# Where VectorE adds, sums and inverts in a two-map attention: halves of a head from PSUM, the pair sum of tiles 0 and 1, both reciprocals behind the turn

## The reference, cut to what matters

```python
q1, q2 = heads(x @ Q1_w.T), heads(x @ Q2_w.T)            # 8 heads of 32, 1024 tokens
k1, k2 = heads(x @ K1_w.T + K1_b), heads(x @ K2_w.T + K2_b)
a1 = softmax(q1 k1^T / sqrt(32));  a2 = softmax(q2 k2^T / sqrt(32))
o = (a1 - lam * a2) @ v                                  # lam: one number per head
# then: normalise o over 4 groups of 64 channels x 1024 tokens, project, add to x
```

## Time and profile before

| | |
|---|---|
| median of 3 runs | 5963.3 us |
| the profiled execution, its own time | 5965.52 us |
| its span | 5963.7 us |
| busy: PE, its weight loads, DVE, ACT, POOL | 97%, 62%, 84%, 55%, 50% |
| PE clock granted, mean | 0.994 of full |

### The profile page before, as it was taken

One profiled execution on the slowest core, in us unless ns is written; L12 is line 12 of the kernel. 1 busy time (PEld: TensorE's weight loads), 2 busy tenths in 40 slices (PEclk: granted clock), 3 DMA queues, 4 the chain that ended last, 5 costly groups with the idle time before them and its releaser, 6 DMA issues.

```text
span 5963.7 us, 117362 instructions
## 1 busy us (share of the span) xinstructions
PE 5762.7 (97%) x39472; PEld 3674.9 (62%) x39472; DVE 5002.4 (84%) x6839; ACT 3258.7 (55%) x5868; POOL 2957.8 (50%) x1334
## 2 busy tenths in 40 slices
PE   6999999999999999999999999999999999999999
PEld 4566565655657556575665756657566575665656
DVE  5978879798897988979889798897978979788797
ACT  4645546455564655646556465564655646555464
POOL 3816538074380744708347183561825628266281
PEclk9999999999999999999999999999999999999999
DMA  2212222122222222222222221222212222122221
GB/s 78 59 48 62 60 55 54 56 58 58 53 52 62 54 58 55 49 61 58 57 55 50 63 58 55 55 51 63 60 49 56 50 63 59 49 60 50 65 59 47
DMA packets 148810, 338.00 MB, mean 57 GB/s; under 512 B 38624, under 2 KB 61280, under 8 KB 139744
## 3 DMA queue, kind: packets, MB, share of 16 engines
q1 hardware_dynamic: 146400, 329.26, 22.7%
q10 hardware_dynamic: 1792, 1.12, 0.1%
HBM read 90.49 MB, written 17.30 MB: 18 GB/s over the span
## 4 chain that ended last, share of the span: by engine, by line
PE 79%; DVE 10%; issue 6%; DMA 2%; ACT 2%; SPq 0%; DVEq 0%; ACTq 0%
PE psum L1141 18%; PE psum L1363 16%; PE psum L1285 15%; PE psum L1306 14%; PE psum L1460 7%; DVE minus_max L834 5%; PE psum L1313 4%; PE psum L1193 1%; PE psum L1332 1%; PE psum L1414 1%; PE psum L1291 1%; DMA prob_sums<-combine_rows_dram 1%; DMA stack<-stage 1%; DVE small L749 1%; DVE small L886 1%
## 5 line engine op out<-in xcount | busy, mean ns | idle before, releaser
L579 ACT ACTIVATE probs<-psum 128x512 f32<-128x512 f32 x4096 | 2215.8, 595 | 1249.8 <-PE psum L1363 1220.1
L423 POOL TENSOR_TENSOR prob_sums<-prob_sums,probs 128x1024 f32<-128x1024 f32 x960 | 2288.2, 2383 | 475.6 <-DVE prob_sums L930 396.2
L834 DVE TENSOR_REDUCE minus_max<-psum 128x1 f32<-128x1024 f32 x2048 | 2397.8, 1206 | 145.7 <-PE psum L1285 132.7
L1363 PE MATMUL psum<-stack 98*128 98x512 f32 x4096 | 1439.1, 431 | 3.5 <-DVE max_rows L844 3.5
L1285 PE MATMUL psum<-stack 96*128 96x512 f32 x4096 | 1219.4, 406 | 39.7 <-DVE minus_max L834 28.9
L1306 PE MATMUL psum<-probs,v_tokens 128*32 128x256 f32 x16384 | 1112.3, 387 | 0.0
L393 POOL TENSOR_TENSOR stage<-probs,stage 128x512 fp32r<-128x512 f32 x16 | 20.7, 1295 | 2130.9 <-ACT probs L545 2130.9
L1363 PEld LDWEIGHTS psum<-stack 98*128 98x128 f32 x4096 | 712.1, 189 | 541.4 <-ACT probs L579 331.6
L1285 PEld LDWEIGHTS psum<-stack 96*128 96x128 f32 x4096 | 713.8, 189 | 324.5 <-DVE minus_max L834 143.5
L1306 PEld LDWEIGHTS psum<-probs,v_tokens 128*32 128x32 f32 x16384 | 453.0, 110 | 468.1 <-issue 227.4
L423 POOL TENSOR_TENSOR prob_sums<-probs 128x1024 f32<-128x1024 f32 x240 | 573.9, 2391 | 273.3 <-ACT probs L579 273.3
(11 more groups left out here) (162 smaller groups left out, 5163.7 us busy)
## 6 DMA issues: line engine op xcount, KB each, us to landing
stack<-stage SPq DMA_DIRECT2D x1024, 128.0 KB, 3.0
stack<-stage SPq DMA_DIRECT2D x256, 256.0 KB, 3.1
prob_sums<-combine_rows_dram SPq DMA_DIRECT2D x128, 256.0 KB, 3.8
stage<-combine_rows_dram SPq DMA_DIRECT2D x128, 256.0 KB, 3.3
x_tile<-x_dram SPq DMA_DIRECT2D x34, 512.0 KB, 3.6
x_tile<-o_head SPq DMA_DIRECT2D x480, 32.0 KB, 1.9
y_dram<-residual SPq DMA_DIRECT2D x16, 512.0 KB, 2.8
y_dram<-stage SPq DMA_DIRECT2D x16, 512.0 KB, 2.9
```

The source lines that it names most:

```text
L423: nc.gpsimd.tensor_tensor(total, first, probs[:, k % NP, :], ALU.add).then_inc(sum_pool, 1)
L579: nc.scalar.activation(probs[:, k % NP, half * HALF:(half + 1) * HALF], ps[:, exp_bank(k) + half, :], ACT.Exp).then_inc(p_ready, 1)
L834: v.tensor_reduce(nm[:, u % 2, q:q + 1], flat_in, AX.X, ALU.max, negate=True).then_inc(ring_free, 1)
L1363: mm(ps[:, exp_bank(k) + half, :], stack[0:KS, s, 1, kt * P:(kt + 1) * P], stack[0:KS, s, 0, half * HALF:(half + 1) * HALF], start=True, s ...
```

## The change

- Each head's second half is written to PSUM, in place, and VectorE adds the first half from there (in place of L399 on POOL). The semaphore `o_free` is split into `o_first`, `o_second`, `oh_ready`.
- `pair_sum(u)` adds tiles 0 and 1 (group 0), beside block 5 of pair 0, in units 0 to 13; in unit 14 it stays with tiles 4 and 5. POOL then adds tiles 2 and 3 on top, and all of group 1.
- In unit 14 tiles 6 and 7 are added by VectorE (`last_sum`), not by POOL. `norm_sums(0)` moves from unit 15 to unit 14, behind `pair_sum`.
- Both halves of the reciprocal stand behind the turn, ahead of block 0 of pair 2. `head_statistics` moves to pair 2 of the odd units.
- ACT and VectorE take the first half of a projection when PE has finished that half (`proj_half`). In unit 0 PE forms a block of the ring ahead of tile 2's scores, and tile 0's values behind them.

```diff
+def pair_group(u):
+    return int(u == UNITS - 2)
+BY_DVE = ((UNITS - 2) * NT + 6, (UNITS - 2) * NT + 7)
 ADDED = [u * NT + kt for u in range(UNITS - 1) for group in sum_groups(u) for kt in group[1:]
-         if kt != sum_groups(u)[1][1]]
-LAST_ADDED = [kt for group in sum_groups(UNITS - 1) for kt in group[1:]]
+         if kt != sum_groups(u)[pair_group(u)][1] and u * NT + kt not in BY_DVE]
+LAST_ADDED = list(BY_DVE) + [(UNITS - 1) * NT + kt for group in sum_groups(UNITS - 1) for kt in group[1:]]
-FIRST_VALUES_AT = ((0,), (1, 2), (3, 4), (5, 6))
+FIRST_VALUES_AT = ((), (1, 2), (3, 4), (5, 6))
-NORM_AT = (UNITS - 1, 0)
+NORM_AT = (UNITS - 1, 1)
...
-                def add_head(h):
-                    pool.wait_ge(o_free, b * UNITS + 2 * h + 2)
-                    nc.gpsimd.tensor_tensor(oh[:, h % 2, :], oh[:, h % 2, :], ot[:, :],
-                                            ALU.add).then_inc(oh_ready, 1)
...
                 def project(t):
-                    act.wait_ge(ring_full, b * len(RING) + RING_AT["proj", t] + 1)
                     for half in range(NH):
+                        if half:
+                            act.wait_ge(ring_full, b * len(RING) + RING_AT["proj", t] + 1)
+                        else:
+                            act.wait_ge(proj_half, b * 3 + t + 1)
...
                 def ring_step(item):
                     n = RING_AT[item]
-                    dve.wait_ge(ring_full, b * len(RING) + n + 1)
+                    if item[0] != "proj":
+                        dve.wait_ge(ring_full, b * len(RING) + n + 1)
...
-                        v.scalar_tensor_tensor(ot[:, :], ps[:, bank, 0:CQ], nlam[:, h:h + 1], rec[:, :],
-                                               ALU.mult, ALU.mult).then_inc(o_free, 1)
+                        v.scalar_tensor_tensor(ps[:, bank, 0:CQ], ps[:, bank, 0:CQ], nlam[:, h:h + 1], rec[:, :],
+                                               ALU.mult, ALU.mult).then_inc(o_second, 1)
+                        dve.wait_ge(o_second, b * HEADS + h + 1)
+                        v.tensor_tensor(oh[:, h % 2, :], ps[:, bank, 0:CQ], oh[:, h % 2, :],
+                                        ALU.add).then_inc(oh_ready, 1)
...
                 def pair_sum(u):
-                    n, k = u * GROUPS + 1, u * NT + sum_groups(u)[1][1]
+                    g = pair_group(u)
+                    n, k = u * GROUPS + g, u * NT + sum_groups(u)[g][1]
...
                 def ahead_of_score(u, kt):
-                    if u % 2 == 0 and u >= 4 and kt == 0:
-                        head_statistics((u - 4) // 2)
                     if u and kt == 4:
+                        sum_recips(u - 1, 0)
                         sum_recips(u - 1, 1)
                 def beside_score(u, kt):
-                    if u and kt == 3:
-                        sum_recips(u - 1, 0)
-                    if u < UNITS - 1 and kt == 5:
+                    if u % 2 and u >= 3 and kt == 5:
+                        head_statistics((u - 3) // 2)
+                    if u < UNITS - 1 and kt == sum_groups(u)[pair_group(u)][1]:
                         pair_sum(u)
+                    if u == UNITS - 2 and kt == 5:
+                        norm_sums(0)
+                    if u == UNITS - 2 and kt == 6:
+                        last_sum(u, 1, 6)
                     if u == UNITS - 1 and kt == NT - 2:
-                        last_sum(1, 5)
+                        last_sum(u, 1, 5)
                     if u and kt == HEAD_AT:
                         head_out(u - 1)
-                    if u == UNITS - 1 and kt == NT - 1:
-                        head_statistics(HEADS - 2)
+                    if u == UNITS - 2 and kt == 7:
+                        last_sum(u, 1, 7)
...
                         for kt in (2 * pair, 2 * pair + 1):
                             k = u * NT + kt
+                            if k == 2:
+                                ring_step(BESIDE[u, pair][0])
...
+                            if k == 2:
+                                weighted(0, 0)
-                            for item in BESIDE[u, pair][slice(0, 2) if kt % 2 == 0 else slice(2, None)]:
+                            for item in BESIDE[u, pair][slice(int(k == 2), 2) if kt % 2 == 0 else slice(2, None)]:
```

More of the change, by code:

```diff
@@ L73, in adds @@
     u, kt = divmod(tile, NT)
-    if u == UNITS - 1:
+    if u == UNITS - 1 or tile in BY_DVE:
         return len(ADDED)
@@ L77, in adds, with last_adds @@
     return sum(at <= u * NT + upto for at in ADDED)
-def last_adds(kt):
-    upto = max([kt] + [group[1] for group in sum_groups(UNITS - 1) if kt == group[0]])
-    return sum(at <= upto for at in LAST_ADDED)
+def last_adds(tile):
+    u, kt = divmod(tile, NT)
+    upto = max([kt] + [group[1] for group in sum_groups(u) if kt == group[0]])
+    return sum(at <= u * NT + upto for at in LAST_ADDED)
 def ones_after(u, pair):
@@ L418, in _ @@
                                 pool.wait_ge(ones_done, b * ONES + n - NS + 1)
-                            if kt > group[1]:
+                            if kt > group[1] and k - 1 in ADDED:
                                 pool.wait_ge(sum_pool, b * len(ADDED) + adds(k) - 1)
@@ L565, in _ @@
                             act.wait_ge(pv_done, b * UNITS * NT + k - NP + 1)
-                            if k == NP or adds(k - NP) > adds(k - NP - 1):
+                            if k > NP and adds(k - NP) > adds(k - NP - 1):
                                 act.wait_ge(sum_pool, b * len(ADDED) + adds(k - NP))
-                            if k >= NT and kt == 0:
+                            if kt == NP and u < UNITS - 2:
+                                act.wait_ge(sum_pair, b * (UNITS - 1) + u + 1)
+                            if k == (UNITS - 1) * NT:
                                 act.wait_ge(sum_pair, b * (UNITS - 1) + u)
-                            if k - NP >= (UNITS - 1) * NT:
-                                act.wait_ge(sum_last, b * len(LAST_ADDED) + last_adds(kt - NP))
+                            if k - NP >= BY_DVE[0]:
+                                act.wait_ge(sum_dve, b * len(LAST_ADDED) + last_adds(k - NP))
                         if k == NP - 1:
@@ L958, in last_sum @@
                     dve.wait_ge(p_ready, b * 2 * UNITS * NT + 2 * k + 2)
-                    if kt == group[1]:
+                    if u < UNITS - 1 and kt == group[2]:
+                        dve.wait_ge(sum_pair, b * (UNITS - 1) + UNITS - 1)
+                    elif kt == group[1]:
                         dve.wait_ge(ones_done, b * ONES + n - NS + 1)
                     else:
-                        dve.wait_ge(sum_last, b * len(LAST_ADDED) + last_adds(kt) - 1)
+                        dve.wait_ge(sum_dve, b * len(LAST_ADDED) + last_adds(k) - 1)
                     first = probs[:, (k - 1) % NP, :] if kt == group[1] else total
-                    v.tensor_tensor(total, first, probs[:, k % NP, :], ALU.add).then_inc(sum_last, 1)
+                    v.tensor_tensor(total, first, probs[:, k % NP, :], ALU.add).then_inc(sum_dve, 1)
                 def k2_low_part():
@@ L988, in _ @@
                             beside_score(u, at)
-                        if (u, pair) == NORM_AT:
-                            norm_sums(0)
                         if u == UNITS - 1:
                             for g, at in (((0, 1),), ((0, 2),), ((1, 4),), ())[pair]:
-                                last_sum(g, at)
+                                last_sum(u, g, at)
                 norm_variance(0)
@@ L1274, in ring_step @@
                                             slice(half * HALF, (half + 1) * HALF))
+                            if half == 0:
+                                last.then_inc(proj_half, 1)
                     elif item[0] == "part":
@@ L1317, in add_up @@
                 def add_up(u, g):
-                    if u == UNITS - 1:
-                        pe.wait_ge(sum_last, b * len(LAST_ADDED) + last_adds(sum_groups(u)[g][-1]))
+                    last = u * NT + sum_groups(u)[g][-1]
+                    if last in LAST_ADDED:
+                        pe.wait_ge(sum_dve, b * len(LAST_ADDED) + last_adds(last))
                     else:
-                        pe.wait_ge(sum_pool, b * len(ADDED) + adds(u * NT + sum_groups(u)[g][-1]))
+                        pe.wait_ge(sum_pool, b * len(ADDED) + adds(last))
                     ones_mm(u, psums[:, (u * GROUPS + g) % NS, :], g == len(sum_groups(u)) - 1).then_inc(ones_done, 1)
@@ L1365, in attention @@
                                    stop=True).then_inc(st_full, 1)
-                            for item in BESIDE[u, pair][slice(0, 2) if kt % 2 == 0 else slice(2, None)]:
+                            if k == 2:
+                                weighted(0, 0)
+                            for item in BESIDE[u, pair][slice(int(k == 2), 2) if kt % 2 == 0 else slice(2, None)]:
                                 if item[0] != "turn":
                                     ring_step(item)
```

(2 more changed lines are left out.)

30 lines of the change are left out of this document (11 added, 19 removed).

## The result

The changed kernel takes 6104.28 us (median of 4 runs, 6102.93 to 6105.52); the kernel before, run beside it, 5964.52 (5961.51 to 5970.19). The ratio is 1.0233, with a 95% interval of 1.0215 to 1.0251. That is 140 us or 2.3% slower, where 6089 was forecast (6015 to 6145).

What follows compares the result with a forecast made beforehand. PE and VectorE were both taken as nearly full, tied by hand-overs. Per image 9.7 + 0.4 + 0.4 + 1.0 - 3.2 - 0.45 = 7.85 us, times 16 = +126, giving 6089 us (6015 to 6145).

Steps and rivals of the forecast that it cites:

- The step from s1 to s3, and from s4 to the turn: Ring blocks s0 to s7 follow each turn: s3's load waits for s1's reduction (4.06); s4 at 7.00, turn done 14.76.
- Rival B: Plain rounds: only the pair sum's place costs, PE makes up the reciprocals' delay; round 13.90, 5965 us; chance 0.07.
- Rival A: VectorE isn't the limit, its extra work falls into waits; plain rounds take PE's 13.50, 5878 us; chance 0.13.
- The size of a plain round: Turn to turn, nine per image: 14.76 us against a mean of 13.68 before, +1.08 each, 9.7 per image.
- Head from PSUM: Product written to PSUM (0.47, 0.57 to next start) and add (0.41) behind s3's reduction: covered by 1.7 us of room, costs nothing.
- 0.69 hold: Long rounds before: pair sum stood still 0.69 us for POOL in rounds with the head's add; forecast to go.
- The three rounds with projections: 52.17 us before; VectorE's idle time was to take most of the cost: +1.0 for all, from 0 to 2.9.
- The last round: Last stretch between turns of an image, no pair sum: from 13.97 to 14.39 us, +0.4.
- The end and the start: End, last turn to projection: about 3.2 us gained (2 to 4); start, halves taken early: 0.6 (0 to 1.0).
- Unit 0's stretch: Its pair sum comes ahead of the turn and costs 0.15 us beyond an idle stretch.
- the same room: VectorE's 1.7 us of room behind s3's reduction, to which the statistics were said to move, with no price given.
- Rival C: POOL meets the pair sum every round if a 0.6 us margin fails: up to 0.69 per round, 6190 us; chance 0.06.

Runs made afterwards that it cites:

- e6: Changed kernel with an extra unused 64-column reciprocal on VectorE right behind the turn, units 1 to 13: 6190.01 us.
- e7: Changed kernel with the same extra reciprocal, units 1 to 13, behind s3's reduction, ahead of head_out: 6103.78 us.
- e1: Changed kernel with the first half of the reciprocal again ahead of the turn, beside tile 3: 6026.44 us.
- e2: Changed kernel with the pair sum again of tiles 4 and 5, between s1 and s2; both reciprocals stay behind the turn: 6059.1 us.
- e3: Changed kernel with both undone: first half of the reciprocal ahead of the turn, pair sum of tiles 4 and 5: 5900.01 us.
- e4: Kernel before with the head's halves added from PSUM and nothing else of the change: 5936.48 us.
- e8: e3 with head statistics back at the start of the even units (last head but one stays in unit 15): 5877.62 us.
- e10: Changed kernel with POOL's last add of a group cut to 512 columns: 6101.04 us.
- e5: e3 with the start of attention as before (whole projection slots, old order in unit 0): 5920.8 us.

## Why the prediction was right, point by point

**The step from s1 to s3, and from s4 to the turn.** Right, and shown: the waits stand where the prediction put them, e6 and e7 tell the two places apart, and e1 and e2 (each half alone) are worth 78 and 45 us. Rival B had the reciprocals' delay made up by PE: in e2, where nothing but the reciprocals is late, plain rounds take 14.16 to 14.50; with the reciprocal back as well (e3) they take 13.45 to 13.70. Rival A, no cost on VectorE, is refuted by the time.

**The size of a plain round.** 14.61 as a mean against 14.76. Of the 0.15, 0.06 is the pair of reciprocals (1.67 against 1.73), 0.03 PE from s3 to s4 (2.91 against 2.94), and some 0.05 the turn, whose cast comes 0.34 to 0.45 behind its load where I took 0.47. Nine rounds make 8.3 instead of 9.7, 22 us too much in the sum.

**Head from PSUM.** The write took 0.48, and 0.52 to the next start; the add 0.42. "So it costs nothing" holds in the changed kernel (0.74 idle behind it). In the faster versions, with little idle time left, the rounds with it are up to 0.2 longer (e4, e8). The 0.69 hold of rounds with the head's add is gone: e4 is faster by 30 us, 24 of them between turns 0 and 15. The rest is in part clock: 6 of its ends are at the lower level, not 12.

**The three rounds with projections.** The term that failed: +3.25 against +1.0, outside its bounds of 0 to 2.9. I had argued that idle time of VectorE would take most of it. Its waits there stand at other places of the round, and idle time takes up only work that stands in front of it. The extra reciprocal behind the turn (e6) costs these rounds 0.4 each, just as it costs the plain ones. With the first half of the reciprocal back ahead of the turn (e1) they take 53.43 instead of 55.42, and with the pair sum back as well (e3) 52.67: 2.0 and 0.75. The term is 36 us too little in the sum. The last round was 0.3 shorter than forecast, the first 0.1 longer, which is the held pair sum that e10 takes away (13.87, where 13.90 was forecast).

**The end and the start.** -3.3 against -3.2 at the end, and that is partly luck. The end that I read took 20.26, with the lower clock behind the 2.44 wait. Against the four images of full clock (18.72) the change gains 2.2; the other 1.16 as a mean is the clock, which the prediction has no term for. So its own terms were 1.0 too large. At the start the halves gave 0.4 of the 0.6 forecast (0.55 by e5 against e3). Unit 0's stretch is +0.1 against +0.15, but of two things of which I had priced one: its pair sum ahead of the turn costs 0.47 (11.43 against 10.96 in e2 and e3), and PE's new order there gives 0.36 back (10.96 in e3, 11.32 in e5).

**The statistics.** They cost 1.3 per image where both other parts are undone (e3 against e8), and the prediction gave them no price: it called their place "the same room". In the changed kernel the rows bear it out. Round 904.88 to 919.53 has them behind s1's reduction:

```profile
907.34 2.37 POOL L422 TENSOR_TENSOR prob_sums<-probs 128x1024 f32<-128x1024 f32 x1 [0.81 <-ACT probs L582]
...
908.76 0.41 DVE L880 BATCH_NORM_STATS2 small<-o_head 128x6 f32<-128x256 f32 x1
```

It takes 14.65, and VectorE still waits 0.94 for PE ahead of s4's reduction; the plain rounds without them take 14.50 to 14.67. So they cost nothing there, and they have a price in e3, where PE comes to s5's load early enough to wait for s3's reduction.

**Rival C.** I gave the hold by POOL a margin of 0.6; it was about 0.4 (POOL's add ends at 999.18, the pair sum begins at 999.57), and it held. With rounds 0.35 shorter (e1) it is lost. The Trainium skill ("SBUF — State Buffer", Who interferes with whom) has the rule, a VectorE instruction with two SBUF inputs against one of GpSimd's that reads SBUF; the 1276 and 1503 ns above agree with it.

**The sum.** +22 too much and 36 too little in two terms, the others within 5 us each: 126 forecast, 139 by the profiled spans. The total is nearer than its parts, which is luck: two errors of opposite sign, and within the end a third that the clock made up for.

## What to carry to other kernels

In a pipeline of two engines tied by a short ring, ask of each side instruction not how long it is but between which two hand-overs it stands: ahead of the reduction that frees a slot, the same short reciprocal in each round cost 86 us, and behind the one before a wait it cost none. Fill the round trips of a turn with work of about the trip's length, and move work only into idle time that lies behind it in the list. And when several parts of a change are late in one round, undo them together as well as singly, since each hides part of the others' price.

## What the runs showed of the hardware that was not expected

Even tiny VectorE instructions on SBUF were held by POOL. In the kernel before, the sums of 8 columns ahead of `norm_groups`, while POOL ran its two adds from 1051.73 to 1056.56:

```profile
1051.81 2.34 DVE L883 COPY small<-small 128x8 f32<-128x8 f32 x1
1054.07 0.16 DVE L885 TENSOR_TENSOR small<-small 128x8 f32<-128x8 f32 x1
1054.26 2.32 DVE L886 SCALAR_TENSOR_TENSOR small<-small 128x8 f32<-128x8 f32 x1
```

In the changed kernel, with POOL at rest, the same copy at 1080.55:

```profile
1080.55 0.16 DVE L887 COPY small<-small 128x8 f32<-128x8 f32 x1
```

Each held one ended within 0.03 of the end of one of POOL's adds (1054.13 and 1056.56), and the one that began as the first of these ended went through in 0.16. The copy has one SBUF input and was held nevertheless. The batch statistics of 256 columns, one SBUF input too, took 0.41 in the middle of one of POOL's adds (908.76 in the changed kernel, above), so they weren't held. The three instructions shown took 4.8 us at the end of attention, for work of 0.5. The Trainium skill ("SBUF — State Buffer", Who interferes with whom) says that a copy can also take the ports shared with GpSimd; the 2.34 agrees.
